# Lookups past the last node read one of 128 stored copies of the last row

## The reference, cut to what matters

```python
NTOKEN, NINP = 25000, 64

def gcn_conv(x, W, b, row, col, num_nodes):
    h = x @ W
    loop = arange(num_nodes)
    row_sl, col_sl = concatenate([row, loop]), concatenate([col, loop])
    deg = segment_sum(ones_like(col_sl), col_sl, num_nodes)
    dinv = rsqrt(maximum(deg, 1.0))
    msg = h[row_sl] * (dinv[row_sl] * dinv[col_sl])[:, None]
    return segment_sum(msg, col_sl, num_nodes) + b

h1 = gcn_conv(emb, W1, b1, row, col, NTOKEN)
lookup = gcn_conv(h1, W2, b2, row, col, NTOKEN)      # 25000 rows of 64 float32
return lookup[input]                                 # input: 512 x 200 asks

# the asks, and how they are drawn:
r_input = randint(key, (512, 200), 78, 199964)
```

## Time and profile before

| | us |
|---|---|
| runs (three) | 7286.15, 7277.15, 7286.85; median 7286.15 |
| the profiled execution, its own time | 7271.66 |
| its span, first to last instruction | 7269.9 |
| issue of the first to the last fetch of the lookup stage (L429) | 6034.3 to 7127.0 |
| last write of `out` issued (L333) | 7265.6 |

### The profile page before, as it was taken

One profiled execution on the slowest core, in us unless ns is written; L12 is line 12 of the kernel. 1 busy time (PEld: TensorE's weight loads), 2 busy tenths in 40 slices (PEclk: granted clock), 3 DMA queues, 4 the chain that ended last, 5 costly groups with the idle time before them and its releaser, 6 DMA issues.

```text
span 7269.9 us, 202878 instructions
## 1 busy us (share of the span) xinstructions
PE 4020.8 (55%) x60793; PEld 3053.1 (42%) x60794; DVE 4445.4 (61%) x12751; ACT 2005.4 (28%) x5160; POOL 4662.6 (64%) x4819
## 2 busy tenths in 40 slices
PE   8977787888888888553455556546556550000000
PEld 5633454555555556543445555446445450000000
DVE  8988898999999998547455656556556551000000
ACT  0037777777777776323000000000000000000000
POOL 0013577777777777774777777777777756776661
PEclk9989999999999999666666767667667675555555
DMA  0001111111111111111211111111111117999998
GB/s 15 0 21 50 37 38 38 40 38 39 39 38 39 39 38 40 39 39 51 51 39 39 39 39 39 39 39 40 39 39 39 39 29 63 40 43 43 43 43 49
DMA packets 167796, 282.10 MB, mean 39 GB/s; under 512 B 79372, under 2 KB 79382, under 8 KB 167120
## 3 DMA queue, kind: packets, MB, share of 16 engines
q0 software_dynamic: 151040, 219.19, 27.2%
q1 hardware_dynamic: 12832, 54.72, 1.9%
q10 hardware_dynamic: 3760, 6.16, 0.3%
HBM read 227.84 MB, written 51.92 MB: 38 GB/s over the span
## 4 chain that ended last, share of the span: by engine, by line
POOL 39%; issue 23%; PE 16%; DVE 10%; DMA 7%; DVEq 2%; ACT 0%; POOLq 0%; SPq 0%; ACTq 0%
POOL scratch L394 29%; POOL acc L429 10%; PE ps L562 8%; PE ps L634 7%; DMA scratch<-table,source 7%; DVE acc L996 3%; DVE late L975 2%; DVE late L986 2%; DVE place_i L953 1%; PE ps L687 1%; DVEq L994 0%; DVE picked L947 0%; DVEq L986 0%; DVE acc L280 0%; POOL scratch L388 0%
## 5 line engine op out<-in xcount | busy, mean ns | idle before, releaser
L394 POOL DMA_INDIRECT scratch<-table,source x3920 | 3753.8, 958 | 1272.5 <-issue 1148.1
L634 PE MATMUL ps<-scratch,late 128*128 x52800 | 2749.1, 214 | 1499.2 <-DMA scratch<-table,source 1369.2
L634 PEld LDWEIGHTS ps<-scratch,late 128*128 128x128 f16 x52800 | 2490.2, 111 | 2016.0 <-issue 1774.0
L996 DVE TENSOR_TENSOR acc<-acc,ps 128x256 f32 x4400 | 1817.2, 413 | 1277.6 <-PE ps L634 1243.6
L986 DVE TENSOR_SCALAR late<-ramp,target 128x512 f16<-128x512 f16 x3850 | 1381.0, 359 | 109.8 <-PE ps L634 85.1
L486 ACT ACTIVATE late<-prt_onehot,scratch 125x128 f16<-125x128 f16 x4000 | 1217.3, 387 | 453.5 <-DVE prt_onehot L809 353.0
L562 PE MATMUL ps<-late 125*128 125x440 f16 x4000 | 1067.9, 357 | 235.0 <-DVE late L975 222.9
L429 POOL DMA_INDIRECT acc<-lookup,ask_i x800 | 755.6, 945 | 361.3 <-issue 338.0
L975 DVE TENSOR_SCALAR late<-ramp,tcol 125x440 f16<-125x440 f16 x2000 | 714.4, 364 | 0.0
L497 ACT ACTIVATE late<-distance,one_col 128x512 f16<-128x512 f16 x550 | 397.0, 722 | 525.4 <-PE ps L634 488.5
L363 POOL CAST scratch<-acc 128x896 bf16 (+1 forms) x14 | 15.2, 1088 | 679.3 <-DVE acc L1075 679.3
(11 more groups left out here) (128 smaller groups left out, 1029.9 us busy)
## 6 DMA issues: line engine op xcount, KB each, us to landing
scratch<-table,source POOLq DMA_INDIRECT x3920
out<-acc SPq DMA_DIRECT2D x40, 640.0 KB, 58.8
table<-scratch SPq DMA_DIRECT2D x28, 672.0 KB, 3.4
acc<-lookup,ask_i POOLq DMA_INDIRECT x800, 117.5
lookup<-acc SPq DMA_DIRECT2D x4, 1568.0 KB, 5.1
late<-embT ACTq DMA_DIRECT2D x47, 128.0 KB, 2.6
scratch<-edge_index SPq DMA_DIRECT2D x2, 976.6 KB
ask_i<-r_input SPq DMA_DIRECT2D x1, 400.0 KB, 16.8
```

The source lines that it names most:

```text
L394: pool.indirect_dma_start(out=place, out_offset=None, in_=table[r], in_offset=bass.IndirectOffsetOnAxis(ap=source[:, t:t + 1], axis=0)).th ...
L634: last = pe.matmul(visit_ps[k][:, n * FEAT:(n + 1) * FEAT], target_onehot[:, k, n * P:(n + 1) * P], row[:, part * FEAT:(part + 1) * FEAT], ...
L996: dve.tensor_tensor(dst, dst, visit_ps[k].rearrange("p (n f) -> p n f", f=FEAT), ALU.add).then_inc(visits_added, 1)
```

## The change

`lookup` gets 128 more rows behind the table. After the four quarters SP copies the sums of node 24,999 (partition 39, tile 195 of `acc`, in the last quarter) into each of these 128 rows with one more DMA, and GpSimd waits for five DMAs in place of four. `find_asked` gets three more steps, between its last step and the target one-hots of pass 1 on VectorE: it computes for each partition p the distance from the last node's row to copy p, multiplies it by (ask >= 25,000), and adds that to the address. So partition p's asks past the last node all read copy p; an ask for exactly 24,999 still reads the original. The copies are 256 B each and lie side by side, 32 KB in all. The values that come out are the same.

```diff
-        lookup = nc.dram_tensor("lookup", [P * NT, FEAT], F32).ap()
+        lookup = nc.dram_tensor("lookup", [P * NT + P, FEAT], F32).ap()
...
+        spare_row = sb("spare_row", [P, 1], F32)
...
-        lookup_v = lookup.rearrange("(p i) f -> p i f", p=P)
+        lookup_v = lookup[0:P * NT, :].rearrange("(p i) f -> p i f", p=P)
...
                 sp.dma_start(lookup_v[:, q * QT:(q + 1) * QT, :], acc[:, q * QT:(q + 1) * QT, :]).then_inc(lookup_written, 16)
+            lp, lt = (NODES - 1) % P, (NODES - 1) // P
+            sp.dma_start(lookup[P * NT:P * NT + P, :].rearrange("(a i) f -> a i f", a=1),
+                         acc[lp:lp + 1, lt:lt + 1, :].broadcast_to([1, P, FEAT])).then_inc(lookup_written, 16)
...
-            pool.wait_ge(lookup_written, 16 * 4)
+            pool.wait_ge(lookup_written, 16 * 5)
...
                 step(dve.scalar_tensor_tensor(ask_i[:, :], ask_t, float(NT), ask_i[:, :], ALU.mult, ALU.add))
 
+                last = (NODES - 1) % P * NT + (NODES - 1) // P
+                step(dve.tensor_scalar(spare_row[:, :], visit_no[:, 0:1], 1.0 / BT, float(P * NT - last), ALU.mult, ALU.add))
+                step(dve.tensor_scalar(ask_f, ask_f, float(NODES), spare_row[:, 0:1], ALU.is_ge, ALU.mult))
+                step(dve.tensor_tensor(ask_i[:, :], ask_i[:, :], ask_f, ALU.add))
...
-ASK_STEPS = 6
+ASK_STEPS = 9
```

## The result

The changed kernel takes 7057.35 us, the median of four runs (7053.06 to 7059.50), against 7286.50 for the kernel before (7277.15 to 7289.51): 0.969 of the time, 95% interval 0.967 to 0.970, or 229 us less. The forecast was 7056.

The account below looks back on a forecast made before the run. DMA engines reading one row bind the lookup stage; relieved, GpSimd binds. Last fetch 7032.3 + 2.8 + 4.3 for the tail + 0.4 for the copy = 7039.8; with 1.8 and 14.5 of offsets, 7056 us, range 7035 to 7100.

Parts of the forecast that it names:

- What bounds the kernel: Lookup stage: DMA engines bind at 1.545 us a fetch, because 112 of 128 rows read are one row, 13.8 ns each.
- The fetches: Lookup stage: packets fall from 1.32 to 0.237 us, so GpSimd's 1.249 us a fetch binds; last fetch starts at 7032.3.
- The edge: Lookup stage: DMA engines stop binding once a packet costs under 1.07 us, so two parts of the memory would do.
- The tail: End of the span: last fetch lands in 2.8 us, SP's last write is issued, span ends 4.3 us later, at 7039.4.
- The copy's DMA: Before the first fetch: the fifth DMA, behind the fourth quarter's, adds 0.4 us, at most 8.5.
- VectorE: Before pass 1's target one-hots: three added steps take 1.75 us, hidden under 9.6 us of cover, cost nothing.
- The sum and the offset: Whole kernel: span 7039.8, plus 1.8 for the execution, plus 14.5 by which the median stood above it: 7056.
- The prediction's signs: Lookup stage: GpSimd's pace has fallen if a fetch is busy above 0.945 us or issue takes above 0.30 us.
- the copies share a place: Rival, lookup stage: all 128 copies are as crowded as the one row, packet stays 1.32 us, 7287; chance 0.08.
- the slower case: Rival, lookup stage: 128 rows in the same part cost more a read, 0.15 us a fetch, 7405; chance 0.03.
- the size of 256 B or the target in `acc` is the cause: Rival, lookup stage: packets are slow through something the fetches keep, so the change brings nothing, 7287; chance 0.03.
- Half a relief: Rival, lookup stage: reads spread unevenly, 1.397 us a fetch, 118 us more than forecast, 7174; chance 0.06.

Follow-up runs that it names:

- e1: The changed kernel with its comparison set to 1,000,000, so that no ask is moved: 10240.8 us against 10226.0 for the kernel before.
- e4: The kernel before with every ask clamped to the last row, 128 of 128 rows of a fetch: 10368.5 us, 143 more than the kernel before.
- e7: The changed kernel with one copy, read by 7 of the 112 asks past the table in a fetch: 10167.0 us against 10119.9 for the changed kernel.
- e2: The changed kernel with two copies 256 B apart in place of 128: 10112.5 us, 128 less than e1 on the same chip.
- e3: The changed kernel with two copies 4 KB apart in place of 128: 10115.2 us, 126 less than e1 on the same chip.
- e6: The changed kernel with two copies 64 KB apart in place of 128: 10059.0 us beside 10162.4 for the kernel before.
- e8: The changed kernel with one slot for fetched rows in place of eight, so GpSimd pauses after each 20 fetches: 10214.6 us.

## Why the prediction was right, step by step

**What bounds the kernel.** Right, and shown by e1, e4 and e7: the DMA engines were held up by the reads of one row. The inference beside it, "one part of the memory that gives 256 B in 13.8 ns", was too large: by e2 a row 256 B away is free of it. The 13.8 ns themselves hold (13.5 in e4). The pauses in the stretch of the earlier trace rows are 4.6 to 8.5 us long, not 5 to 8; nothing hung on it.

**The fetches.** The price of a packet was put at 0.237 us, by pass 1's rows, and was 0.127; the forecast share of 0.25 was 0.166. Nothing hung on it. The edge, "under 1.07 us" a packet, was thought out wrongly, because it took the packet's length for a cost when it was a wait; two copies would have sufficed all the same. GpSimd's pace, 1.249, was measured as 1.248.

**The tail.** Forecast 2.8 + 4.3 = 7.1 us after the start of the last fetch, measured 7051.3 - 7041.9 = 9.4. The step that failed is which queue ends last. The fetch landed and SP issued its write at 7044.2, 2.3 us after the fetch's start (forecast 2.8), and the write had landed 3.0 us later; but the span ended with GpSimd's queue, whose drain ran from 7027.9 to 7051.1. In the kernel before the same drain ended at 7269.7, only 0.8 us after SP's own end at 7268.9, so that the 4.3 us of the earlier trace rows could be read as SP's.

**The copy's DMA.** Forecast 0.4 us, measured 1.2: from the first scaling to the first fetch 43.1 us against 41.9 before. Its line in the trace, L331:

```profile
L331 SPq DMA_DIRECT2D lookup<-acc x1: 928/928/928, 6034.4 to 6034.4; - x1
...
DMA to landing us min/median/max: 9.2/9.2/9.2
```

**VectorE.** Forecast 1.75 us, hidden; measured 0.15 + 0.64 + 0.99 = 1.78, and not quite hidden. Timeline of the changed kernel, to be held against the earlier trace rows:

```profile
3477.27 0.15 DVE L937 TENSOR_SCALAR spare_row<-visit_no 128x1 f32<-128x1 f32 x1
3477.46 0.64 DVE L938 TENSOR_SCALAR late<-late,spare_row 128x800 f32<-128x800 f32 x1
3478.13 0.99 DVE L939 TENSOR_TENSOR ask_i<-ask_i,late 128x800 int32<-128x800 int32 x1
3478.47 1.49 POOL L399 DMA_INDIRECT scratch<-table,source  x1 [7.71 <-DMA table<-scratch]
```

The target one-hots are in time, as forecast. But the last step runs beside GpSimd's first gather, which takes 1.49 us in place of 1.05: 0.4 us on the path, since TensorE starts on the first batch 12.1 us after the first gather's start, before 11.7. The prediction had not looked for this overlap; that it is the cause was not tested.

**The sum and the offset.** The forecast for the span was 7039.8 and it was 7051.3, 11.5 more: 0.8 for the copy, 2.3 for the tail, less 0.6 for the pace, and 9.0 that had been lost before the last sum. The most of that is in the sorting before pass 0: the first gather starts at 817.2, before at 808.6. Whether that is scatter or a cost is open. For scatter: the version with VectorE scaling had 806.9 and 817.8 on two chips, and the medians' 229 us against the lookup stage's 227.6 leave no room for a loss. For a small cost: the nine other traces of kernels with the added steps have 814.4 to 825.5, and e4, without them, 806.4; and on the experiments' chips some 5 us are missing from the medians. On the other side the 14.5 us by which the median stood above the profiled execution were carried over whole, and after the change it stands 7057.35 - 7053.06 = 4.3 above. So 11.5 too little and 10.2 too much came out at 1.35 us from the result. The mechanism and its size are confirmed, the closeness is luck. So is GpSimd's pace: the 1.249 held in the first measurement, and on the experiments' chips the same kernel takes 1.364 us a fetch and saves half as much. The prediction's signs name a fall of the pace, but its range goes no further than 1.263.

**The rivals.** That the copies share a place fell with e2, e3 and e6, and with them the slower case, which hung on it. That the size of 256 B or the target in `acc` is the cause fell with the result itself, which kept both, and that a by-product is, with e1. Half a relief isn't seen: no fetch waits for a slot. The rule of the Trainium skill on transfers under 512 B (DMA: Bandwidth & Descriptors, Specifications) had been set aside by a row; the relief at an unchanged 256 B agrees. The prediction had stretched what the Trainium skill states there of row pitches at large powers of two (Latency and other measured facts) to steps of 256 B; that reading fails, for copies 256 B, 4 KB and 64 KB apart are equally quick here (0.168, 0.184 and 0.177 us a packet). Row pitches as large as those it gives, 512 KiB and more, no run here has.

## What to carry to other kernels

Look at which addresses an indirect DMA reads, not only at how many and how large: clamped or padded indices all fall on one row, and engines line up at it while the profile shows busy DMA engines and small rates. A few copies, even side by side, dissolve the line, as long as no row keeps more reads than it can give in the time of a fetch. And when a stage has been freed, price the next bound at its sustained pace, with its queue's drain, for here both ate into the gain.

## What the runs showed of the hardware

- One 256 B row in HBM, read by all DMA engines at once, gives a read in 12 to 14 ns (112 reads in 1.545 us, 105 in 1.455, 128 in 1.734), and the packets' time is then nearly all waiting: 1.32 us against 0.17 with two rows and 0.115 with sixteen.
- GpSimd's time for a fetch rose from 945 to 1095 ns after some 250 us of work without pause in the experiments' runs, and stayed at 945 where a pause of 5 us came after each 20 (e8). In e4 it fell from 1.09 back to 0.95 us with the first pause, of 2.0 us. In the first profile of the changed kernel it stayed at 944 ns for 1,000 us without a pause.
- GpSimd's queue drains late: 8.3 us after its last fetch in the changed kernel, 17 where its pace had slowed, and 1.9 us in e8, with pauses (last fetch 10207.1 + 0.9, drained at 10209.9). What it waits for no run shows.
- A float32 operation of VectorE on 128 x 3136 that takes 3.4 us alone took 8.55 and 10.0 beside one of GpSimd, and ended 3.3 us after it both times.
